# A gated feed-forward kernel: block products in another order, one wide maximum, the closing sums on GpSimd, rounding on VectorE

## The reference

```python
# x: (2, 2048, 512), cond_8: (2, 8), cond weight: (8, 512, 512), gate and up: (2048, 512), down: (512, 2048)
w_bot = einsum('bg,got->bot', cond_8, weight * mask)
h = einsum('bnt,bot->bno', x, w_bot) + bias
# bitlinear: activations rounded to 8 bits per row, weights to -1, 0, 1 by their mean
def _act_quant(x):
    scale = 127.0 / clip(max(abs(x), axis=-1), 1e-05)
    return clip(round(x * scale), -128, 127) / scale
gate = silu(_bitlinear(h, w_gate))
up = _bitlinear(h, w_up)
return x + _bitlinear(gate * up, w_down)
```

## Time and profile before

| | us |
|---|---|
| median of 3 runs | 485.14 (484.19 to 487.47) |
| the profiled execution | 484.49 |
| its span, first to last instruction | 482.7 |
| its mean granted TensorE clock | 0.996 of full |

### The profile page before, as it was taken

The page is one execution under the profiler, slowest core; times in us unless marked ns, Lnnn a source line. Parts: engine busy times, 40 slices in busy tenths (PEclk is TensorE's granted clock), DMA queues, the critical chain, the costliest instruction groups (busy, mean ns, idle before and its releaser), DMA issues.

```text
span 482.7 us, 7229 instructions
## 1 busy us (share of the span) xinstructions
PE 452.9 (94%) x2184; PEld 234.4 (49%) x2222; DVE 359.5 (74%) x743; ACT 295.5 (61%) x412; POOL 92.4 (19%) x83
## 2 busy tenths in 40 slices
PE   4899999999998999999999999999999999999967
PEld 0234444444443555564555555555555555555543
DVE  0324979898677888787888887878878787888872
ACT  1227586873557757676665667676666767666660
POOL 0000434241750011120211112020211112021120
PEclk9999999999999999999999999999999999999999
DMA  7999978956204344525363342435344242536424
GB/s 290 404 399 417 369 216 233 365 131 132 44 7 82 71 94 126 132 43 135 73 132 88 97 130 44 130 63 147 66 116 118 56 130 49 147 66 132 113 62 130
DMA packets 104311, 69.76 MB, mean 145 GB/s; under 512 B 87264, under 2 KB 87264, under 8 KB 102752
## 3 DMA queue, kind: packets, MB, share of 16 engines
q1 hardware_dynamic: 103712, 67.39, 50.8%
q10 hardware_dynamic: 576, 2.10, 1.2%
HBM read 40.11 MB, written 8.39 MB: 100 GB/s over the span
## 4 chain that ended last, share of the span: by engine, by line
PE 32%; issue 21%; ACT 20%; DVE 17%; DMA 8%; DVEq 0%; ACTq 0%; SPq 0%
PE ps L618 13%; PE ps L649 12%; ACT wc L344 8%; DVE wc L534 7%; ACT wc L333 5%; PE ps L674 4%; DMA wc<-w_gate 4%; ACT w_bot L351 3%; DMA qT<-q_sb 3%; DVE wc L488 2%; DMA wc<-wcond 2%; PE ps L683 2%; PE ps L631 1%; ACT tern_up L311 1%; DVE p_unit L558 1%
## 5 line engine op out<-in xcount | busy, mean ns | idle before, releaser
L649 PE MATMUL ps<-tern_gate,qT 128*128 128x512 bf16 x482 | 127.1, 379 | 10.4 <-DVE wc L534 7.9
L534 DVE TENSOR_TENSOR wc<-ps,wc 128x512 f32<-128x512 f32 x128 | 88.2, 689 | 57.1 <-ACT wc L333 51.9
L649 PE MATMUL ps<-tern_up,qT 128*128 128x512 bf16 x504 | 129.8, 379 | 0.4
L618 PE MATMUL ps<-w_bot,xT_sb 128*128 128x512 f32 x256 | 113.2, 595 | 2.3 <-DVE w_bot L428 1.6
L338 ACT ACTIVATE wc<-wc,p_scale 128x1024 f32<-128x1024 f32 x62 | 67.8, 1141 | 65.0 <-DVE p_scale L563 65.0
L333 ACT ACTIVATE wc<-ps,gate_unit 128x512 f32<-128x512 f32 x128 | 83.8, 683 | 36.2 <-PE ps L649 36.2
L536 DVE TENSOR_REDUCE p_part<-wc 128x1 f32<-128x512 f32 x128 | 87.8, 686 | 4.4
L649 PEld LDWEIGHTS ps<-tern_up,qT 128*128 (+1 forms) x512 | 50.1, 98 | 60.4
L618 PEld LDWEIGHTS ps<-w_bot,xT_sb 128*128 128x128 f32 x256 | 48.0, 190 | 61.2 <-issue 57.5
L649 PEld LDWEIGHTS ps<-tern_gate,qT 128*128 (+1 forms) x512 | 48.6, 97 | 57.6 <-issue 22.7
L344 ACT ACTIVATE wc<-wc 128x1024 f16<-128x1024 f32 x64 | 64.0, 1054 | 3.1 <-DVE wc L572 3.1
(11 more groups left out here) (61 smaller groups left out, 254.4 us busy)
## 6 DMA issues: line engine op xcount, KB each, us to landing
xT_sb<-xT SPq DMA_DIRECT2D x32, 256.0 KB, 7.2
x_res<-x SPq DMA_DIRECT2D x30, 256.0 KB, 2.7
out<-result SPq DMA_DIRECT2D x30, 256.0 KB, 2.1
wc<-wcond SPq DMA_DIRECT2D x12, 512.0 KB, 13.8
...
```

Of the source, the lines that this page charges most:

```text
L534: nc.vector.tensor_tensor(cut, ps[:, UP + c % 2], silu[:, c % 2], ALU.mult).then_inc(prod_ready, 1)
L618: ins = nc.tensor.matmul(ps[:, t % COND_BANKS], xT_sb[:, t % XSLOTS, k], w_bot[:, t // HALF, k], start=(k == 0), stop=(k == KH - 1))
L649: ins = nc.tensor.matmul(ps[:, bank + c % 2], tile, w[:, c, k], start=(k == 0), stop=(k == KH - 1))
```

## The change

- **Block products.** An odd step issues three of them (new numbers 0 to 2, behind chunks 1 to 3), an even step four (3 to 6, behind chunks 0 to 3). The order is now X, Z, V, X, Z, V, Z by bank. ScalarE copies parts behind products 0, 1, 2 and 4, placed anew among its other work.
- **Wider maximum.** The product of each chunk stays, but the maximum of chunks 0 to 2 is one instruction over 1536 columns, and chunk 3 has its own. One small instruction joins both with a floor computed ahead for all tiles (`p_floor`, two more instructions in `units`). Then a reciprocal and a scaling, three small ones in place of five.
- **Rounding.** VectorE rounds both halves at the end of each step; ScalarE's `round_half` is gone.
- **Finishing.** `out_unit` of each tile and all closing work except `finish_c11` go to GpSimd: two scalings and two sums with x per pair. VectorE does the two joins with PSUM (`join_blocks`) in the next odd step.
- **Stores.** The first tile of a pair is stored ahead of the transposes of an odd step, the second behind them.
- **Tail.** `down_plain` of tile 30 stands ahead of the last two block products.

```diff
...
+    def store(t):
+        par = t % 2
+        sp.wait_ge(result_ready, t + 1)
+        sp.dma_start(out[t], result[:, par]).then_inc(s_store[par], 16)
+        if t + 2 < LATE:
+            sp.dma_start(x_res[:, par], x[t + 2]).then_inc(s_xres[par], 16)
 
     for s in range(1, TILES):
         if s % 2 == 1 and s >= 5:
-            store_pair((s - 5) // 2)
+            store(s - 5)
         transpose_q2(s - 1)
+        if s % 2 == 1 and s >= 5:
+            store(s - 4)
...
+    def unit_of(t):
+        pool.wait_ge(p_col, 3 * t + 1)
+        nc.gpsimd.tensor_scalar(out_unit[:, t:t + 1], p_max[:, t % 2:t % 2 + 1], up_step[:, t:t + 1], w_mean[:, 2:3],
+                                ALU.mult, ALU.mult).then_inc(unit_done, 1)
+
+    def join_parts(j):
         pool.wait_ge(part_out, 4 * j + 3)
-        nc.gpsimd.tensor_tensor(mid[:, 0], part[:, 2], part[:, 1], ALU.subtract).then_inc(mid_done, 1)
-        pool.wait_ge(mid_done, 4 * j + 1)
+        nc.gpsimd.tensor_tensor(mid[:, 2], part[:, 2], part[:, 1], ALU.subtract).then_inc(mid_done, 1)
+        pool.wait_ge(part_out, 4 * j + 4)
+        nc.gpsimd.tensor_tensor(mid[:, 0], part[:, 3], part[:, 1], ALU.subtract).then_inc(mid_done, 1)
+        pool.wait_ge(mid_done, 4 * j + 2)
         if j > 0:
             pool.wait_ge(c12_done, j)
         nc.gpsimd.tensor_tensor(mid[:, 1], mid[:, 0], part[:, 0], ALU.add).then_inc(mid_done, 1)
-        pool.wait_ge(part_out, 4 * j + 4)
-        nc.gpsimd.tensor_tensor(mid[:, 2], part[:, 3], part[:, 1], ALU.subtract).then_inc(mid_done, 1)
+
+    def finish_pair(j):
+        t0, t1 = 2 * j, 2 * j + 1
         pool.wait_ge(c21_done, j + 1)
-        pool.wait_ge(mid_done, 4 * j + 3)
         nc.gpsimd.tensor_tensor(block_sum[:, 2], block_sum[:, 1], mid[:, 2], ALU.add).then_inc(mid_done, 1)
+        pool.wait_ge(c12_done, j + 1)
+        nc.gpsimd.tensor_scalar(block_sum[:, 0], block_sum[:, 0], out_unit[:, t0:t0 + 1], 1.0, ALU.mult, ALU.mult
+                                ).then_inc(sum_scaled, 1)
+        pool.wait_ge(sum_scaled, 2 * j + 1)
+        pool.wait_ge(s_xres[0], 16 * j + 16)
+        if j > 0:
+            pool.wait_ge(s_store[0], 16 * j)
+        nc.gpsimd.tensor_tensor(result[:, 0, NB:HID], block_sum[:, 0], x_res[:, 0, NB:HID], ALU.add
+                                ).then_inc(result_ready, 1)
+        pool.wait_ge(mid_done, 4 * j + 4)
+        second = block_sum[:, 1:3].rearrange("p i n -> p (i n)")
+        nc.gpsimd.tensor_scalar(second, second, out_unit[:, t1:t1 + 1], 1.0, ALU.mult, ALU.mult
+                                ).then_inc(sum_scaled, 1)
+        pool.wait_ge(sum_scaled, 2 * j + 2)
+        pool.wait_ge(s_xres[1], 16 * j + 16)
+        if j > 0:
+            pool.wait_ge(s_store[1], 16 * j)
+        nc.gpsimd.tensor_tensor(result[:, 1], second, x_res[:, 1], ALU.add).then_inc(result_ready, 1)
+
+    for t in range(TILES):
+        unit_of(t)
+        if t == LATE + 1:
+            join_parts(PAIRS - 1)
+        elif t >= 3 and t % 2 == 1:
+            join_parts((t - 3) // 2)
+        elif t >= 4:
+            finish_pair((t - 4) // 2)
+    finish_pair(PAIRS - 1)
...
-    def round_half(t, par, half):
-        act.wait_ge(p_col, 5 * t + 4)
-        cut = prod[:, par, 1024 * half:1024 * half + 1024]
-        nc.scalar.activation(cut, cut, ACT.Copy, bias=ROUND, scale=p_scale[:, par:par + 1]).then_inc(p_rounded, 1)
...
-        act.wait_ge(down_psum, 7 * j + (1, 2, 4, 5)[i])
+        act.wait_ge(down_psum, 7 * j + (1, 2, 3, 5)[i])
         if j > 0 and i == 0:
             act.wait_ge(mid_done, 4 * j)
-        nc.scalar.activation(part[:, i], ps[:, (X, Z, Z, V)[i], 0:NB], ACT.Copy).then_inc(part_out, 1)
+        nc.scalar.activation(part[:, i], ps[:, (X, Z, V, Z)[i], 0:NB], ACT.Copy).then_inc(part_out, 1)
 
     def step(s):
-        odd, par = s % 2, 1 - s % 2
-        if s >= 4 and not odd:
-            copy_part((s - 4) // 2, 2)
+        par = 1 - s % 2
+        odd = (s - 3) // 2 if s >= 3 and s % 2 == 1 else None
+        even = (s - 4) // 2 if s >= 4 and s % 2 == 0 else None
         silu_chunk(s, 0)
-        if s > 0:
-            for half in range(2):
-                round_half(s - 1, par, half)
+        if even is not None:
+            copy_part(even, 1)
         silu_chunk(s, 1)
-        if s >= 4 and not odd:
-            copy_part((s - 4) // 2, 3)
-        if s >= 3 and odd:
-            copy_part((s - 3) // 2, 0)
-            copy_part((s - 3) // 2, 1)
         if s > 0:
             for half in range(2):
                 convert(s - 1, par, half)
+        if odd is not None:
+            copy_part(odd, 0)
+        if even is not None:
+            copy_part(even, 2)
         silu_chunk(s, 2)
+        if even is not None:
+            copy_part(even, 3)
         if s in (1, 2):
             cond_round(LATE + s - 1)
         silu_chunk(s, 3)
...
-        nc.vector.tensor_scalar(up_step[:, cut], h_unit[:, cut], w_mean[:, 1:2], 1.0 / QMAX, ALU.mult, ALU.mult
+        dve.wait_ge(units_ready, 4 * half + 2)
+        nc.vector.reciprocal(step_inv[:, cut], up_step[:, cut]).then_inc(units_ready, 1)
+        dve.wait_ge(units_ready, 4 * half + 3)
+        nc.vector.tensor_scalar(p_floor[:, cut], step_inv[:, cut], FLOOR / QMAX, None, ALU.mult
                                 ).then_inc(units_ready, 1)
...
+    def join_blocks(j):
+        first = isinstance(j, int) and j == 0
+        dve.wait_ge(down_psum, 7 * j + 7)
+        if not first:
+            dve.wait_ge(result_ready, 2 * j)
         nc.vector.tensor_tensor(block_sum[:, 1], ps[:, Z, 0:NB], part[:, 0], ALU.add).then_inc(c21_done, 1)
...
+        dve.wait_ge(mid_done, 4 * j + 3)
...
+    def product(s, par, c):
+        dve.wait_ge(silu_ready, 4 * s + c + 1)
+        dve.wait_ge(up_psum, 4 * s + c + 1)
+        if c == 0 and not (isinstance(s, int) and s < 2):
+            dve.wait_ge(q2_ready, 2 * s - 2)
+        nc.vector.tensor_tensor(prod[:, par, 512 * c:512 * c + 512], ps[:, UP + c % 2], silu[:, c % 2], ALU.mult
+                                ).then_inc(prod_ready, 1)
+
+    def largest(s, par, i, lo, hi):
+        dve.wait_ge(prod_ready, 4 * s + hi)
+        nc.vector.tensor_reduce(p_part[:, par, i:i + 1], prod[:, par, 512 * lo:512 * hi], AX.X, ALU.max,
+                                apply_absolute_value=True).then_inc(part_ready, 1)
 
     def step(s, par, late=None, j=None, b0=0):
...
+        b1 = b0 + 1
+        product(s, par, 0)
+        if j is not None and par == 1 and not (isinstance(j, int) and j == 0):
+            join_blocks(j - 1)
+        if j is not None and par == 0:
+            add_blocks(j, 3, b0, b1)
+        product(s, par, 1)
+        if late is not None:
+            cond_tile(late)
+        if j is not None and par == 1:
+            add_blocks(j, 0, b0, b1)
+            add_blocks(j, 1, b0, b1)
+        if j is not None and par == 0:
+            add_blocks(j, 2, b0, b1)
+            finish_c11(j, s - 4)
+        product(s, par, 2)
+        largest(s, par, 0, 0, 3)
+        product(s, par, 3)
+        largest(s, par, 1, 3, 4)
+        if not (isinstance(s, int) and s < 2):
+            dve.wait_ge(unit_done, s - 1)
+        dve.wait_ge(part_ready, 2 * s + 2)
+        nc.vector.tensor_scalar(p_max[:, par:par + 1], p_part[:, par, 0:1], p_part[:, par, 1:2], column(p_floor, s),
+                                ALU.max, ALU.max).then_inc(p_col, 1)
+        dve.wait_ge(p_col, 3 * s + 1)
+        nc.vector.reciprocal(p_inv[:, par:par + 1], p_max[:, par:par + 1]).then_inc(p_col, 1)
+        dve.wait_ge(p_col, 3 * s + 2)
+        nc.vector.tensor_scalar(p_scale[:, par:par + 1], p_inv[:, par:par + 1], QMAX, None, ALU.mult
                                 ).then_inc(p_col, 1)
-
-    def round_last():
-        dve.wait_ge(p_col, 5 * TILES - 1)
+        dve.wait_ge(p_col, 3 * s + 3)
         for half in range(2):
-            cut = prod[:, 1, 1024 * half:1024 * half + 1024]
-            nc.vector.tensor_scalar(cut, cut, p_scale[:, 1:2], ROUND, ALU.mult, ALU.add).then_inc(p_rounded, 1)
+            cut = prod[:, par, 1024 * half:1024 * half + 1024]
+            nc.vector.tensor_scalar(cut, cut, p_scale[:, par:par + 1], ROUND, ALU.mult, ALU.add
+                                    ).then_inc(p_rounded, 1)
...
-        if i in (0, 1, 4) and not first:
-            pe.wait_ge((c11_done, c21_done, None, None, c12_done)[i], j)
-        if i == 0:
-            pe.wait_ge(s_q2T[0], 32 * j + 16)
-        elif i == 1:
-            pe.wait_ge(s_q2T[1], 32 * j + 32)
-        elif i == 2:
-            pe.wait_ge(part_out, 4 * j + 1)
-        elif i == 3:
-            pe.wait_ge(part_out, 4 * j + 2)
-            pe.wait_ge(sum_ready, 4 * j + 2)
-        elif i >= 5:
+        if i < 3 and not first:
+            pe.wait_ge((c11_done, c21_done, c12_done)[i], j)
+        if i < 2:
+            pe.wait_ge(s_q2T[i], 32 * j + 16 + 16 * i)
+        if i >= 3:
             pe.wait_ge(part_out, 4 * j + i - 2)
```

(44 more changed lines are left out.)

92 lines of the change are left out of this document (21 added, 71 removed).

## The result

| | before | after |
|---|---|---|
| median of 4 runs | 485.21 us (484.19 to 487.47) | 464.74 us (464.14 to 465.26) |
| ratio after / before, 95% interval | | 0.957 [0.954, 0.961] |
| profiled execution | 484.49 | 465.11 |
| its span | 482.7 | 463.3 |

A forecast was written before the change was run, and what follows sets the result against it. TensorE bounds the kernel, idling 23.5 us from step 3 on. 23.5 - 0.84 (steps 0 to 3) - 0.8 (end) = 21.9 off 484.49 gives 462.6; median 0.65 above, 463.2; with the tight place's allowance 464.6 us, range 460.5 to 472.

The forecast's parts named there:

- all 1.37 us a pair: Loop of the kernel before: TensorE stands still 1.37 us of each 21.31 us pair, waiting for VectorE's late product.
- Dense at 19.94: Steady pair: 16 halves and 7 block products on TensorE without a gap take 19.94 us.
- the tight place: Odd step's product 0 on VectorE, after the even step's roundings: starts 2.8 us in, may start at 3.44, 0.65 in hand.
- the allowance of 0.1 for each of fourteen pairs: Added to the 463.2 us sum for the tight place, out of 0 to 0.3 us a pair, giving 464.6 us.
- the sign named ahead for the ports: VectorE's sums of blocks: any over 0.69 us would show VectorE and GpSimd meeting at their shared ports.
- The stall before chunk 2 of step 3: Step 3: product 0 comes at 161.1 where chunk 2 wants it by 159.7, a stall of 1.65 us.
- the 1.07 us that I let step 3 gain: Steps 2 to 3: product 2 now ahead of chunk 0, so step 3 starts at 155.76 instead of 156.83.
- I expect no idle: Tail: TensorE never waits, as tile 31's transposes land near 17.4 and are needed at 18.2; 5.8 us gained.
- Loss 0.8 (0 to 1.5): End: by way of GpSimd's last finishing and the last pair's store the span ends at 24.2 instead of 23.4 us.
- A: Rival: ports or the tight place cost more than is in hand; pair 20.3 to 20.8, 469 to 476 us; 16%.
- C: Rival: VectorE, held by GpSimd instructions, becomes the bound; 22.2 us a pair, 496 us; 6%.
- B: Rival: GpSimd 2 us late delays silu 2 and the next rounding on ScalarE; pair back at 21.3, 483 us; 4%.

The follow-up runs named there:

- e1: After kernel with the rounding back on ScalarE, both halves behind silu 0 of the next step (last tile's stays on VectorE): 471.14 us, ratio 0.970.
- e3: Kernel before with only the rounding moved from ScalarE to VectorE, at the end of each step: 472.49 us, ratio 0.973.
- e5: After kernel plus two spare 512-column VectorE maxima behind the roundings, in each even step from 4 on: 474.77 us; in odd steps instead: 465.35 us.
- e6: After kernel plus a spare 512-column GpSimd sum just ahead of the roundings of each even step from 4 on: 465.99 us, ratio 0.960.
- e6b: After kernel plus a longer spare GpSimd sum, 1024 columns f16, just ahead of the roundings of each even step from 4 on: 480.02 us, ratio 0.987.
- e10: e9 with the sum over w_down's absolute values two tiles later (tile 23 instead of 21): 465.25 us, ratio 0.957.
- e9: e7 with GpSimd's joins of the last pair waiting until tile 31 is rounded: 461.67 us, ratio 0.950.
- e7: After kernel with the second half of `units` behind step 5, step 31's transposes ahead of the store, last pair's closing on VectorE: 464.28 us, ratio 0.956.

## Why the prediction was right, point by point

**The bound.** TensorE's idle time behind late products was named as what could be won, and it is what was won: 20.6 us between step 3 and the last matmul, to which the front adds 0.4 and from which the end takes 1.7. e1 and e3 show that the cause was put half right. I laid the late product to ScalarE's order. Taking only ScalarE's rounding away (e3) left the pair at 20.30 us with VectorE full, and leaving the rounding on ScalarE in the new order (e1) still won most. Two queues were in the way, and each of the two measures cures most of the pair. The prediction also overlooked one wait. It put all 1.37 us a pair on the late product, but 0.36 of them stood in the odd step ahead of a block product, for a part copied out by ScalarE (1.22 us from start to start where 0.86 is dense). In the kernel before:

```profile
310.75 1.03 PE L649 MATMUL ps<-tern_up,qT 128*128 128x512 bf16 x4
311.97 1.05 PE L674 MATMUL ps<-tern_down,wc 128*128 128x256 f16 x8 [0.19 <-ACT w_bot L351]
```

That wait went with the others. It bears on ScalarE's order too, so the forecast didn't suffer.

**The steady pair.** Dense at 19.94, measured 19.93. The wide maximum 1.75 (1.76), the rounding 0.753 at the median of 64 (0.75), `finish_c11` and joins as before, VectorE 17.77 us a pair (17.7), ScalarE 10.2 (11.2). Product 0 of the odd step at 2.97 (2.8 to 3.1), with 0.47 in hand where I had 0.65. e5 shows this to be the tight place, and the allowance of 0.1 for each of fourteen pairs was not needed: it measured 0.

**GpSimd.** The groups by shape from 200 to 450 us (count, busy us, mean ns), beside the earlier trace rows:

```profile
L333 POOL TENSOR_TENSOR result<-w_bot,x_res 128x512 f32<-128x512 f32 x13 | 16.5, 1271 | 1.1
L323 POOL TENSOR_TENSOR result<-w_bot,x_res 128x256 f32<-128x256 f32 x13 | 13.6, 1042 | 1.1
L317 POOL TENSOR_SCALAR w_bot<-w_bot,out_unit 128x256 f32<-128x256 f32 x13 | 12.9, 993 | 0.0
...
L327 POOL TENSOR_SCALAR w_bot<-w_bot,out_unit 128x512 f32<-128x512 f32 x13 | 8.9, 688 | 0.0
```

The 512-column sum is 1.27 (1.20 from the line through two rows), the 512-column scaling 0.69 (0.53 to 0.8). The 256-column ones are 0.99 and 1.04 in the loop but 0.48 and 0.72 in the tail, where no `add_blocks` runs beside them: in the loop it is GpSimd that is held. VectorE's 60 sums keep a median of 0.682 us, but the second one of each odd step takes 0.77: the sign named ahead for the ports (over 0.69) came, with 0.09 us a pair, and product 2 behind it had room. In sum GpSimd works 7.6 us a pair where 6.1 and two tiny ones were laid out, and is done about 8.9 us into the odd step (9), with nobody waiting in the loop. The rule of the Trainium skill (SBUF — State Buffer, "Who interferes with whom") that whichever starts first keeps the shared ports for its whole instruction agrees with the lines of e6, e6b and e10; it gives no price for the after kernel. One row of the loop doesn't fit it as it reads: GpSimd's 256-column scaling is shown starting 0.05 us ahead of VectorE's first sum (322.83 and 322.88), yet the scaling takes 0.99 instead of 0.48 and the sum its usual 0.68. Whether that is the rule failing or a start time off by a little is open.

**Steps 0 to 3.** The stall before chunk 2 of step 3 was sized 1.65 and measured 1.84 (162.97 against 161.13 if dense), that before chunk 1 0.26 and 0.37. Step 2 to step 3 takes 7.17 us (7.35) where it took 8.42. But step 2 itself starts at 149.26 instead of 148.41, so of the 1.07 us that I let step 3 gain it gains 0.40. That loss of 0.85 is nearly all there before the main stage begins, at the matmul that waits for `w_up`'s sum:

```profile
71.92 0.35 PE L721 MATMUL ps<-abs_sum,ones 128*128 128x4 f32 x2 [0.76 <-ACT tern_up L352]
```

In the kernel before it stands at 71.16. The change touches nothing ahead of it, and other executions put it elsewhere (71.81 in e9, 72.17 in e7, and 71.65 in e3, which up to there is the kernel before), so I don't lay it to the change.

**The tail.** The low clock and the waits went, as said. Two terms were mis-sized. "I expect no idle" failed by 0.67 us (299.0 + 0.37 + 1.84 make 301.21 of 301.88): the transposes of tile 30 were to be issued 7.3 us into step 31 and came 8.5 in, since the store waited for GpSimd's sum until 6.9 (6.5 laid out), its 256-column instructions being held as above, and the x load's issue took 1.13 us:

```profile
444.51 0.34 SPq L247 DMA_DIRECT2D out<-result  x1
444.90 1.13 SPq L249 DMA_DIRECT2D x_res<-x  x1
446.13 2.60 SPq L241 DMA_TRANSPOSE wc<-wc  x2
```

"Loss 0.8 (0 to 1.5)" was 1.66. VectorE and GpSimd in order of time, in the tail:

```profile
448.73 0.73 POOL L304 TENSOR_TENSOR w_bot<-w_bot 128x256 f32<-128x256 f32 x1
448.75 2.40 DVE L600 TENSOR_SCALAR wc<-wc,p_scale 128x1024 f32<-128x1024 f32 x2
...
458.14 1.26 POOL L333 TENSOR_TENSOR result<-w_bot,x_res 128x512 f32<-128x512 f32 x1
```

and SP's last issues:

```profile
457.42 2.36 SPq L247 DMA_DIRECT2D out<-result  x2
459.82 0.91 SPq L269 DMA_DIRECT2D out<-h_sb  x2
```

GpSimd's last sum ends at 459.40, 1.1 us behind TensorE's last matmul, where I had 1.2 (the terms written there sum to 21.1, not 21.3). The term that was wrong is what follows it: I let the span end 2.9 us after that sum (24.2 - 21.3), and it ended 3.9 after. The stores of tiles 30 and 31 stand behind the last pair's in SP's order: they are issued from 459.82 to 460.73, though the result of tile 31 was ready at 459.10, and the term has no room for those two issues: one issue of 0.35 and 2.4 us to landing already make 2.8 of its 2.9. The 2.40 us of the roundings, 1.42 elsewhere, are a hold by GpSimd's joins that the prediction's tail didn't have either, but TensorE lost nothing by it in this kernel: it is dense from 452.95 on.

**The sum.** 21.9 us off the span were forecast, 19.4 came: 0.67 less from the start of step 3, 0.30 from its stalls, 0.67 from the transposes in the tail, 0.86 from the end. These 2.5 us took the place of the 1.4 us that I had added for the tight place, which cost nothing, and of 1.0 us of offset: I put the median 0.65 above the profiled execution, and it was 0.37 below it (464.74, 465.11). So that 464.6 stands beside 464.74 is luck in the last 2.5 us: the pair was right to 0.01 us, the ends were 2.5 us too good, the allowance 1.4 us too much.

**The rivals.** A and C (ports) have a mechanism that exists and cost TensorE nothing in the pairs here: e6b reached 480.02 with one GpSimd instruction of 2.12 us a pair at the wrong place. B did not show: no wait of TensorE for a copied part is left in the pair.
